# Two edits to TensorE's program: a prefetch hint on its loops' jumps back, and the 64-row and 32-row convolution taps interleaved

## What is computed

```
spec = inverse_fft(modes of fft(h), mixed by complex weights)   # 16 x 16 modes
conv = 3 x 3 convolution of h, padding 1, with bias
h    = leaky(spec + conv)
```

## Time and profile before

| | |
|---|---|
| median of 3 runs | 8086.82 us (8085.25 to 8110.36) |
| the profiled execution, its own time | 8098.54 us |
| its span, first to last instruction | 8096.7 us |
| granted TensorE clock, mean | 0.924 of full |
| TensorE matmuls busy | 6837.6 us (84%), 120694 records |
| TensorE weight loads busy | 4060.7 us (50%) |
| VectorE / ScalarE / GpSimd busy | 4950.5 (61%) / 2232.6 (28%) / 63.0 us (1%) |
| L612 matmuls | 18432 records, 1151.4 us busy |
| L619 matmuls | 18432 records, 653.8 us busy |
| queue of instruction fetches | 814 packets, 13.34 MB |

### The profile page before, as it was taken

One profiled execution on the slowest core, in us unless ns is written; L12 is line 12 of the kernel. 1 busy time (PEld: TensorE's weight loads), 2 busy tenths in 40 slices (PEclk: granted clock), 3 DMA queues, 4 the chain that ended last, 5 costly groups with the idle time before them and its releaser, 6 DMA issues. The chain is left out here.

```text
span 8096.7 us, 285876 instructions
## 1 busy us (share of the span) xinstructions
PE 6837.6 (84%) x120694; PEld 4060.7 (50%) x120694; DVE 4950.5 (61%) x7875; ACT 2232.6 (28%) x3074; POOL 63.0 (1%) x46
## 2 busy tenths in 40 slices
PE   4699986989889699989878999966888888888888
PEld 3566665555555555555554444433344444444443
DVE  2599993666666376666636777756455454454554
ACT  1133321222222122222212222223333333333333
POOL 1000000000000000000000000000000000000000
PEclk7799997999999799999979999978999999999999
DMA  6677775444444544444452222220000000000000
GB/s 182 136 134 135 137 141 147 115 116 115 117 116 114 153 120 116 116 117 115 114 158 69 72 72 72 72 67 3 1 3 3 1 3 3 1 3 3 1 3 2
DMA packets 714748, 641.00 MB, mean 79 GB/s; under 512 B 334881, under 2 KB 583841, under 8 KB 705831
## 3 DMA queue, kind: packets, MB, share of 16 engines
q1 hardware_dynamic: 713800, 626.58, 31.8%
HBM read 353.72 MB, written 285.56 MB: 79 GB/s over the span
## 5 line engine op out<-in xcount | busy, mean ns | idle before, releaser
L612 PE MATMUL zbank<-rows_in,conv_taps 64*32 64x512 f32 (+1 forms) x18432 | 1151.4, 642 | 239.5 <-issue 239.5
L966 DVE SCALAR_TENSOR_TENSOR rows_out<-zbank,conv_bias,work 128x1024 f32<-128x1024 f32 x512 | 633.8, 1279 | 1159.8 <-PE zbank L619 1143.5
L568 PE MATMUL abank<-inv_basis,mode_tile 128*32 128x128 f32 x32768 | 1014.8, 276 | 91.6 <-DMA mode_tile<-m_img 54.9
L834 ACT ACTIVATE turned<-tbank 128x1024 f32<-128x1024 f32 x400 | 410.1, 1025 | 2260.3 <-PE tbank L631 2260.3
L568 PEld LDWEIGHTS abank<-inv_basis,mode_tile 128*32 128x32 f32 x32768 | 884.6, 111 | 255.2 <-issue 254.8
L648 PE MATMUL zbank<-fwd_basis,turned 128*32 128x128 f32 x24576 | 756.1, 274 | 106.2 <-DVE rows_out L966 68.7
L612 PEld LDWEIGHTS zbank<-rows_in,conv_taps 64*32 64x32 f32 x18432 | 381.6, 114 | 919.6 <-issue 905.2
L648 PEld LDWEIGHTS zbank<-fwd_basis,turned 128*32 128x32 f32 x24576 | 682.6, 111 | 128.6 <-issue 127.4
L619 PE MATMUL zbank<-rows_in,conv_taps 32*32 32x512 f32 (+1 forms) x18432 | 653.8, 595 | 6.1 <-issue 6.1
L973 DVE SCALAR_TENSOR_TENSOR rows_out<-rows_out 128x1024 f32<-128x1024 f32 x512 | 601.7, 1217 | 0.0
L1559 PE MATMUL banks<-constants 128*128 128x512 f32 x1040 | 520.8, 654 | 22.4 <-issue 22.4
(11 more groups left out here) (356 smaller groups left out, 7672.5 us busy)
## 6 DMA issues: line engine op xcount, KB each, us to landing
h_rows<-rows_out SPq DMA_DIRECT2D x768, 256.0 KB, 3.8
rows_in<-h_rows SPq DMA_DIRECT2D x384, 512.0 KB, 4.9
m_img<-rows_out SPq DMA_DIRECT2D x32, 1024.0 KB, 5.4
mode_tile<-m_img SPq DMA_DIRECT2D x512, 64.0 KB, 3.0
g_half<-modes_out SPq DMA_DIRECT2D x384, 64.0 KB
spectra<-g_half SPq DMA_DIRECT2D x12, 1856.0 KB, 27.3
rows_in<-x_slots SPq DMA_DIRECT2D x96, 194.9 KB
rows_out<-x_slots SPq DMA_DIRECT2D x96, 194.9 KB
```

Of the source, the lines that this page charges most:

```text
L568: last = nc.tensor.matmul(ab[32 * p:32 * p + 32, s, 128 * k:128 * k + 128], mode_tile[u][:, k, a, :], inv[:, k, s, 128 * p:128 * p + 128], ...
L612: nc.tensor.matmul(section(zb[32 * p:32 * p + 32, 2 * a + so, :])[:, :, :, out], conv_t[part, dx, so, :], moving(part, p, 0, src), start=( ...
L834: nc.scalar.activation(turned[q][:].rearrange("p x b n -> p x (b n)"), tb[:], ACT.Identity)\
L966: nc.vector.scalar_tensor_tensor(out=rows_out[u][:, half].rearrange("p (s x) -> p s x", s=2), in0=zb[:, 2 * a:2 * a + 2, :], scalar=conv_b ...
```

## The change

TensorE's loops at L204, L212 and L2887 are built with a hint for their jump back: one more sequencer instruction at the head of each round, which names the branch at its end. The loops at L813, L2882 and L2885 and those of other engines stay as they are. In `pe_conv` the loop over the column shifts goes outside: for every dx first the 64-row taps for so = 0 and so = 1, then the 32-row taps; the wait for g_ready stands ahead of so = 1 of the first shift. The accumulation into each bank still starts with dx = 1 of the 64-row taps and ends with dx = 2 of the 32-row ones.

```diff
+        def looped(eng, start, end):
+
+            return nc.Fori(start, end, engines=bass.OrderedEngineSet([eng.engine]),
+                           hint_back_edge=eng.engine == mybir.EngineType.PE)
+
         def over_layer(eng, body):
 
             body(0)
-            with eng.Fori(1, NP - 1) as i:
+            with looped(eng, 1, NP - 1) as i:
                 body(i)
             body(NP - 1)
...
             body(0)
             body(1)
-            with eng.Fori(2, NP - 1) as i:
+            with looped(eng, 2, NP - 1) as i:
                 body(i)
             body(NP - 1)
...
-            for so in range(2):
-                if so == 1 and kind != "last":
-                    pe.wait_ge(g_ready, ET + n - 1)
-                    pe.nop(nofuse=True)
-                for dx, out, src in SHIFTED:
+            for dx, out, src in SHIFTED:
+                for so in range(2):
+                    if so == 1 and dx == 1 and kind != "last":
+                        pe.wait_ge(g_ready, ET + n - 1)
+                        pe.nop(nofuse=True)
                     for p in range(4):
                         for a in range(2):
                             part = slice(64 * a, 64 * a + 64)
                             nc.tensor.matmul(section(zb[32 * p:32 * p + 32, 2 * a + so, :])[:, :, :, out],
                                              conv_t[part, dx, so, :], moving(part, p, 0, src), start=(dx == 1), stop=False)
-            for dx, out, src in SHIFTED:
                 for p in range(4):
                     for a in range(2):
                         for s in range(2):
...
-            with pe.Fori(0, ITERS) as it:
+            with nc.Fori(0, ITERS, engines=bass.OrderedEngineSet([pe.engine]), hint_back_edge=True) as it:
                 for stage in STAGES:
```

## The result

The changed kernel takes 8156.32 us (median of 6 runs, 8137.45 to 8164.09) against 8092.33 us for the kernel before on the same chip (8085.25 to 8118.60): ratio of the means 1.007, 95% interval 1.0051 to 1.0089. It is **slower by 0.7%**. The forecast was 8057 us. The time lies inside the predicted range (7950 to 8165), but on the side to which 0.28 was given.

What follows compares the result with a forecast made beforehand. TensorE was taken to bound the middle layers, losing 6.3 us a round at jumps back. Terms -79 - 26 - 22 + 12 + 76 + 9 = -30 on 8098.54 gave 8069, then 8057 from the runs' lower median; range 7950 to 8165.

Steps and rivals of the forecast that it cites:

- the side to which 0.28 was given: Whole kernel: the change makes it slower, chance 0.28; faster by over 0.3% had 0.52, within that 0.2.
- What bounds the kernel: Middle layers: TensorE bounds, and 6.3 us a round are lost at its jumps back, 58 times.
- bodies past some size between 1440 and 1856: TensorE's loops: bodies over that many matmuls and weight loads lose their head from instruction memory, giving branches of median 4.3 us.
- The split of the 6.3 us: Middle-layer rounds: of the 6.3 us lost, about 4.1 are the branch and 2.1 the clock.
- The hint in the middle layers: Middle-layer jumps back: shorter branches, -79 us, and less loss behind them, -26 us.
- the first term, -79: Middle-layer branches: the hint shortens them to 2.5 to 3.1 us, worth -79 us.
- the first rival: Middle-layer branches: lead too short, they stay over 3.3 us, at most the useless fetch goes; 8117 to 8162, chance 0.20.
- The second term: Behind the middle-layer branches: the 2.1 us clock loss becomes 1.65 with the second block's stall, -26 us (0 to -52).
- The hint elsewhere: Block loop: first work starts earlier, -22 us; hint's own costs, +12; layer 0 and last layer gain nothing.
- the +12: Hinted loops: 6 us for the hint's extra instruction at the head, 6 for useless fetches where loops end.
- The interleaving, +76: Convolution: six segments instead of two cost 0.39 us a pair in tile changes, over 192 pairs.
- The wait for g_ready, +9: Convolution: the wait moves from behind 48 matmul records to behind 16, holding queued loads; 0.07 x 128 (0 to 40).

Runs made afterwards that it cites:

- run 3: Hint-alone kernel (convolution's old order) with the heads of TensorE's tokenizer loops placed on the first instruction of a 16 KB block: 7758.35 us, 0.9585 of the kernel before.
- slot 144: As run 3, but with the tokenizer loops' heads 144 instructions into a 16 KB block: 7755.33 us, 0.9579 of the kernel before.
- slot 160: As run 3, but with the tokenizer loops' heads 160 instructions into a 16 KB block: 8036.56 us, 0.9926 of the kernel before.
- run 4: As run 3, with the loops' heads at the start of a block, but no hint on any loop: 8149.96 us, 1.0070 of the kernel before.
- run 12: The kernel before with the hint on the block loop (L2887) alone: 8077.88 us, 0.998 of the kernel before.
- run 5: As run 3, with the convolution's new interleaved order: 7841.89 us, 0.9688 of the kernel before.
- run 11: Hint-alone kernel with only the wait for g_ready moved, to behind 16 weight loads instead of 48: 8044.23 us, 0.9930 of the kernel before.
- run 9: As slot 160, with the hint and the convolution's new interleaved order: 8155.92 us, 1.0062 of the kernel before.
- run 2: The kernel before with only the convolution's new interleaved order, no loop hinted: 8208.26 us, 1.0137 of the kernel before.
- slot 239: As run 3, but with the tokenizer loops' heads 239 instructions into a 16 KB block: 8186.95 us, 1.0112 of the kernel before.

## Why the prediction went wrong, step by step

**What bounds the kernel: right, with one size misread.** TensorE's jumps back in the middle layers cost 6.3 us a round; run 3 removes them, a round falls from 42.08 to 35.95 us, and the whole gains 336 us, the block loop's part included. But "bodies past some size between 1440 and 1856" was the wrong variable. The body of 1901 instructions can stay (no fetch in run 3); it must touch no more than eight blocks (a branch of 0.216 us at slot 144, a median of 3.33 at slot 160), and the head must not be displaced (4.32 without the hint, run 4). At 7.4 blocks a body at an arbitrary place can touch nine; the 9.6 fetches a round were the clue.

The split of the 6.3 us, 4.1 for the branch and 2.1 for the clock, is an estimate: no run shows the 2.1 as the clock's alone. What the runs show in its place: in the kernel before the first convolution of a round took 10.65 us and the second 8.57, 2.08 less, and the clock granted to the convolution of the earlier trace rows that starts at 3016.28, then to the first 3.39 us of the one behind the gap, was 1.00 and 0.50:

```profile
3016.28:3021.61 5.33, 5.33 (x110) 1.79 (x113) 4.87 (x5) 0.38 (x1) 0.00 (x0) 1.00 0.44 103
3038.31:3041.70 3.39, 3.39 (x33) 0.94 (x34) 1.13 (x1) 0.00 (x0) 0.00 (x0) 0.50 0.98 233
```

The clock's own records have it at half from 3037.16 to 3043.99, so it fell inside the gap, which starts at 3034.23.

**The hint in the middle layers, -79 - 26 = -105: the step that failed.** Measured by the hint alone: (1179.33 - 1149.48) + (1177.06 - 1146.91), where the first of each is the same 28 rounds in the kernel before:

```profile
1449.67:2629.00 1179.33, 1064.57 (x25994) 681.28 (x25989) 786.88 (x784) 251.21 (x281) 0.00 (x0) 0.95 0.45 116
2909.68:4086.74 1177.06, 1063.28 (x25993) 683.65 (x25987) 786.88 (x784) 251.15 (x281) 0.00 (x0) 0.95 0.45 116
```

That is -60 us in 56 rounds, -62 for all 58: 43 us short. What failed is the first term, -79. The prediction took the hinted fetch to start where the first of two fetches had started, 0.25 us behind the branch's start, and the branch to fall to 2.75 us on average. The traces show that the first fetch went and the second stayed. Before, the last fetch inside the 58 branches starts at a median of 1.02 us; with the hint alone the only one starts at 1.00 (0.21 to 1.53), and just 19 of 58 start sooner than 0.9. The gain came from another place: of the branches before, 36 hold two fetches, the second of which takes 1.9 us, and last 4.51 us on average; 22 hold one, which takes 1.0, and last 3.52. With the hint all are of the second kind, 3.38. The mean went from 4.13 to 3.38, and the time from a branch's start to the first matmul from 4.69 to 4.03: 0.66 x 58 = 38 us where 79 stood. This is the mechanism of the first rival ("the lead is too short... at most the useless fetch falls away"), which gave 8117 to 8162; its chance of 0.20 was too low, and its own mark, branches over 3.9, too high.

The second term came out, at 0.40 x 58 = 23 us for 26 (the first convolution went from 10.65 to 10.25), but by luck: it was worked out for branches of 2.75 us, no row stood behind the half of the clock's loss, and the 34th load of the earlier trace rows comes 3041.67 - 3037.76 = 3.9 us behind the branch's end, not "some 3".

**The hint elsewhere, -22 + 12: right within what can be told.** The block loop by itself gives -17 (7 to 24), with L1549 coming 3.2 us earlier behind the jump shown, where 2.9 to 3.3 was worked out. There the fetch that belongs to the branch starts 19.6 to 23.4 us ahead of it in run 12; in the kernel before it starts behind the branch's start (0.92 and 1.01 us at the branches of 6502.5 and 6821.5). Of the +12, neither half was measured apart. The 0.1 us for the hint's own instruction stands on no row, and the trace after has 0.031 to 0.040. The 6 us for the loops' ends are an estimate too: behind the last jump of either middle layer the hint alone has no stall in the first convolution, which takes 5.33 us for its 96 matmuls, as at full clock in the earlier trace rows.

**The interleaving, +76: the size off, and a term missing.** The segments are as costed: 2989.57 to 2992.54, 2.97 us for one 64-row and one 32-row segment, where the prediction had 1.86 + 1.12 = 2.98.

```profile
2989.57 1.92 PE L617 MATMUL zbank<-rows_in,conv_taps 64*32 64x504 f32 x32
2991.42 1.19 PE L623 MATMUL zbank<-rows_in,conv_taps 32*32 32x504 f32 x32
2992.54 1.92 PE L617 MATMUL zbank<-rows_in,conv_taps 64*32 64x504 f32 x32
```

So the undisturbed pair grew by 0.36 (0.39 forecast). In the last layer an ordinary pair grew by 0.46, and the drops of the clock, which no step of the prediction has, bring it to 0.8: 0.4 x 64 = 26 us more. Beside the hinted long branches the order costs 1.24 us a round, where the forecast had 0.78 and 0.14 for the wait: 0.32 x 58 = 19 us more. Taken alone the interleaving is worth +111 us (0.0137 x 8095), not +85 with the wait. At full clock four more changes of tile cost 0.36 us a pair, where four times the 0.13 that the prediction read for one of them would be 0.52; the rest of the 111 has other causes.

**The wait for g_ready, +9: right where nothing stalls.** In run 5 the middle pairs, which have the wait, grew by 0.36, and the ordinary last-layer pairs, which have none, by 0.46; run 11 puts it at about 10 us beside hinted long branches, with an interval of some 20 us to either side.

**The sum.** The ratios split the change in two: 0.9917 with the hint alone and 1.0070 with both are -67 us for the hint and +124 for the order upon it, +57 together. (The spans of the three profiles give -69 and +108; the changed kernel's profile is its fastest run.) The forecast had -115 (-79 - 26 - 22 + 12) and +85, together -30. It failed by 48 us on the hint and by 39 on the order; each error alone would have left it within 20 us of no change, and together they turned the sign.

**What stays open.** Why the order costs half a microsecond a round more beside a hinted long branch (1.24 and 1.30 against 0.72) and not, by its one profile, beside an unhinted one (0.71). Neither the coincidence of the second block with the change of tile (run 9) nor the earlier wait (run 11) accounts for it alone. That loads don't run ahead across a change of tile, so that a late block is felt in full, fits the timeline above (2.37 us between loads against 0.82), but is argued, not shown. That each change takes longer at the lower clock does not fit run 2, whose first convolutions ran at a clock no higher (0.81 against 0.85 in the changed kernel) and grew by 0.26. Nor is it shown what in the interleaved order brings the clock down in the last layer and not in the middle ones.

## What to carry to other kernels

Before you count on a branch hint, count blocks, not instructions: where first and last instruction of a loop's body lay within eight fetch blocks of 16 KB, hint and placement together brought the jump from 4.3 to 0.22 us (about 4% of the kernel, faster than either kernel of this study, with the fetches gone from the DMA view); one block more, and the hint is worth a fraction (0.8% here, the block loop's 0.2 included). With only 17 instructions of the round in the head's block the hinted kernel was slower than the one before (1.0112); what that slot costs without the hint was not run. An order of matmuls that alternates tile shapes paid for its changes here, 0.36 us a pair in the middle layers and 0.46 in the last, and in the last layer almost as much again in drops of the clock. When two edits pull in opposite directions, price each with a run of its own: -0.8% and +1.4% were hidden in a +0.7%.

## What was not expected of the hardware

- A granted clock that falls without a longer pause: in the interleaved last layer about one pair in four or five ran its first 3.4 us at 0.58, and took 19.10 instead of 17.45 us. With the old order this layer ran at 1.00 throughout; with four segments at 0.99 (7 stretches of 3.4 us at half clock); with six at 0.98 (12 or 13), with or without the hint.
- A useless instruction fetch inside a branch went with a longer useful one: this one started 1.0 us behind the branch's start either way, but took 1.9 us where two were inside and 1.0 where it was alone.
- The hint as a keeper rather than a prefetcher: in a body of eight blocks it took the fetches from nine a round to none. Without it the placed body was even slower than the unplaced one (1.0070).
- A shorter branch can make a longer round: at slot 239 the branch fell from 3.33 to 2.69 us against slot 160 and the round rose from 40.8 to 43.4.
